# Weight preparation behind the experts: loads and ternary rounding in the experts' tail, transposes partly between the first scores

## The reference

```
x += tanh(g_xattn[0]) * L0_xattn(layernorm(x), ctx)   # small attention
x += tanh(g_ffn[0])   * L0_ffn(layernorm(x))          # 64 routed experts, top 4, and 2 shared ones
x += tanh(g_xattn[1]) * L1_xattn(layernorm(x), ctx, ctx)  # 32 query heads of 8, keys and values of ctx
x += tanh(g_ffn[1])   * L1_ffn(layernorm(x))          # rmsnorm, causal attention of 16 heads, gated MLP
x += tanh(g_xattn[2]) * L2_xattn(ctx, layernorm(x))
x += tanh(g_ffn[2])   * L2_ffn(layernorm(x))          # ternary weights
x += tanh(g_xattn[3]) * L3_xattn(layernorm(x), ctx, ctx)  # 16 heads, projection Wc
x += tanh(g_ffn[3])   * L3_ffn(layernorm(x))          # soft mixture of experts
```

## Time and profile before

| | us |
|---|---|
| median of 3 runs | 1261.07 (1260.91 to 1263.65) |
| profiled execution | 1259.72, of which the span 1257.9 |
| busy in the span | PE 1044.5, PEld 667.9, DVE 742.0, ACT 524.7, POOL 328.0 |
| stretch of the weight preparation and the start of attention A | about 403 to 454 |

### The profile page before, as it was taken

One profiled execution on the slowest core, in us unless ns is written; L12 is line 12 of the kernel. 1 busy time (PEld: TensorE's weight loads), 2 busy tenths in 40 slices (PEclk: granted clock), 3 DMA queues, 4 the chain that ended last, 5 costly groups with the idle time before them and its releaser, 6 DMA issues.

```text
span 1257.9 us, 18978 instructions
## 1 busy us (share of the span) xinstructions
PE 1044.5 (83%) x6622; PEld 667.9 (53%) x6625; DVE 742.0 (59%) x1684; ACT 524.7 (42%) x883; POOL 328.0 (26%) x626
## 2 busy tenths in 40 slices
PE   4369999999998688877988899991464878999997
PEld 2258888888887432333455435650322434566575
DVE  6875554444443577787565212479697674784743
ACT  1223233333333556565554430233473553544543
POOL 7023434343333456435343200001310300000000
PEclk9659999999999768999999899795686799999999
DMA  6101121111310400000000300002000000000000
GB/s 151 42 1 39 38 50 42 46 46 42 117 25 1 142 2 2 2 3 2 3 3 4 118 1 1 1 1 51 1 2 1 3 2 1 1 9 1 9 10 9
DMA packets 62444, 32.09 MB, mean 26 GB/s; under 512 B 47104, under 2 KB 61072, under 8 KB 62112
## 3 DMA queue, kind: packets, MB, share of 16 engines
q1 hardware_dynamic: 62368, 31.10, 9.3%
HBM read 29.64 MB, written 1.05 MB: 24 GB/s over the span
## 4 chain that ended last, share of the span: by engine, by line
PE 69%; DVE 21%; ACT 4%; issue 3%; POOL 1%; DMA 1%; SPq 0%; POOLq 0%; DVEq 0%; ACTq 0%; PEldq 0%
PE bank L762 16%; PE bank L778 8%; PE bank L874 4%; PE bank L1160 3%; DVE mx L2272 3%; PE bank L989 2%; PE bank L1341 2%; PE bank L957 2%; PE bank L1358 2%; PE bank L919 2%; PE bank L1343 2%; PE bank L1092 2%; PE bank L1140 2%; PE bank L1193 1%; DVE mxc L2272 1%
## 5 line engine op out<-in xcount | busy, mean ns | idle before, releaser
L2272 DVE TENSOR_REDUCE mx<-bank 128x2 f32<-128x512 f32 (+1 forms) x176 | 117.7, 689 | 71.0 <-PE bank L1092 35.1
L1708 ACT ACTIVATE prob<-bank 128x512 f32<-128x512 f32 x176 | 102.9, 597 | 89.3 <-PE bank L1140 62.1
L1520 ACT ACTIVATE hhi<-hh 128x512 fp32r<-128x512 f32 x72 | 45.5, 632 | 153.1 <-DVE hh L2108 140.4
L2104 DVE TENSOR_TENSOR hu<-bank,sg 128x512 f32<-128x512 f32 x64 | 44.3, 692 | 97.1 <-PE bank L762 97.1
L762 PE MATMUL bank<-xh,wh 128*128 128x512 f32 x288 | 91.6, 399 | 0.0
L762 PE MATMUL bank<-xh,wl 128*128 128x512 f32 x288 | 90.5, 395 | 0.0
L762 PE MATMUL bank<-xlo,wh 128*128 128x512 f32 x288 | 90.1, 394 | 0.0
L2096 DVE TENSOR_TENSOR hlo<-hh,hhi 128x512 fp32r<-128x512 f32 x72 | 57.2, 794 | 50.7 <-ACT hhi L1520 50.7
L2704 POOL TENSOR_TENSOR wl<-wraw,wh 128x512 fp32r<-128x512 f32 x72 | 80.6, 1119 | 13.0 <-POOL wh L2701 13.0
L1585 ACT ACTIVATE sg<-bank 128x512 f32<-128x512 f32 x72 | 43.1, 598 | 61.9 <-PE bank L762 61.9
L762 PEld LDWEIGHTS bank<-xh,wh 128*128 128x128 f32 x288 | 54.6, 190 | 13.3 <-issue 0.3
(11 more groups left out here) (456 smaller groups left out, 2275.0 us busy)
## 6 DMA issues: line engine op xcount, KB each, us to landing
wraw<-in_L_ffn_wg_dram SPq DMA_DIRECT2D x64, 64.0 KB, 2.3
wraw<-in_L_ffn_wu_dram SPq DMA_DIRECT2D x64, 64.0 KB, 2.4
wraw<-in_L_ffn_wd_dram SPq DMA_DIRECT2D x32, 128.0 KB, 2.4
l_raw<-in_L_ffn_w_dram SPq DMA_DIRECT2D x2, 1024.0 KB, 6.8
mun<-in_L_ffn_mu_dram SPq DMA_DIRECT2D x1, 2048.0 KB, 7.6
xs<-in_x_dram SPq DMA_DIRECT2D x1, 1024.0 KB, 5.5
w1s<-in_L_ffn_W_dram SPq DMA_DIRECT2D x2, 512.0 KB, 7.7
stage<-in_L_ffn_W_in_base_dram SPq DMA_DIRECT2D x1, 1024.0 KB, 7.8
```

What stands on the lines that cost most here:

```text
L1520: return act.activation(dst, src, ACT.Copy, scale=scale)
L1708: act.activation(t.prob[k][:, :], bank[3 + n % 2][:, :], ACT.Exp).then_inc(S("probs"), 1)
L2104: tt(hu[k % 2][:, :], bank[4 + (n + 1) % 4][:, :], sg[k % 2][:, :], ALU.mult).then_inc(once("up_used"), 1)
L2272: V.reduce_max(out_, bank[n % 3][:, :].rearrange("p (h t) -> p h t", h=heads), AX, negate=True)\
```

## The change

- The stage tiles get room of their own behind the experts' tiles (the memory of the first stage), and SP loads all of them as soon as the last shared expert's load is issued; one semaphore, `stage_loaded`, counts all eight.
- ACT's loop is one turn shorter, the eight units of the tail are written out behind it, and the two sums of magnitudes stand before units 0 and 1. PE's product with ones stands in unit 1. DVE's scale stands in unit 2 and its six rounding passes one each behind units 2 to 7. `tern` moves to the memory of `at_f`.
- POOL's clearing memsets and the parts of the first keys no longer wait for the last `down`.
- The transposes use banks 3 to 5 in turn. The first twelve groups stand before the attention. Four more (wupT) stand in a new slot -4, behind `xn` on ACT. The eight of wdT stand one behind each `by_query` of slot -2, the twelve ternary ones two behind each of the first six of slot -1, and the product for `wa` behind the seventh.
- `prepared` and the last copies are waited for by the first `by_key` instead of ahead of the attention; DVE copies `wa` at the end of slot -1, behind the maxima.

The diff, cut to what the above names (`...` where lines are left out):

```diff
-        top[0] = region
-        top[0] += DC * TOKENS * 4
+        top[0] = after_experts + 8192
         stage = [sb(f"stage{k}", [P, 2048]) for k in range(4)]
         wo = sb("wo", [P, DC, D])
-        after_prep = max(top[0], after_experts + 8192)
-        top[0] = region
-        tern = [sb(f"tern{k}", [P, 2048], BF16) for k in range(2)]
+        after_prep = top[0]
...
+        tern_at = top[0]
         at_f = sb("at_f", [P, B, NT, D])
+        top[0] = tern_at
+        tern = [sb(f"tern{k}", [P, 2048], BF16) for k in range(2)]
...
+        PREP_BANKS = (3, 4, 5)
+        PREP_AT = {"first": range(12), (-4, 0): range(12, 16)}
+        for n in range(8):
+            PREP_AT[-2, n] = range(16 + n, 17 + n)
+            PREP_AT[-1, n] = range(24 + 2 * n, 26 + 2 * n) if n < 6 else range(30 + n, 31 + n)
+        assert PREP_AT[-1, 6] == range(len(PREP + PREPB), len(PREP + PREPB) + 1)
+        del PREP_AT[-1, 7]
+        def prep_bank(g):
+            return PREP_BANKS[g % len(PREP_BANKS)]
...
-            sp.wait_ge(once("hidden_used"), 2 * PAIRS + 4)
-            sp.wait_ge(once("experts_out"), 2 * HALVES)
+            sp.wait_ge(once("batch_arrived"), 3)
...
-            stg = once("stage_rest_loaded")
...
                     up((u + 1) // 2, (u + 1) % 2, T * 8 + u + 1, T * SLOTN + (u + 1) // 2, shared=True)
+                if u == 1:
+                    pe.wait_ge(once("abs_sums"), 2)
+                    mm(bank[4][:, 0:2], ones[:, :], st[:, 0:2], start=True, stop=True).then_inc(once("abs_total"), 1)
                 down(u // 2, u % 2, T * 8 + u, T * SLOTN + u // 2, last_pair=u // 2 == SLOTN - 1)
...
-            pe.wait_ge(once("xs_updated"), 4)
-            pe.wait_ge(once("abs_sums"), 2)
-            mm(bank[4][:, 0:2], ones[:, :], st[:, 0:2], start=True, stop=True).then_inc(once("abs_total"), 1)
-            pe.wait_ge(once("stage_loaded"), 5 * 16)
-            for g, (srcs, dst) in enumerate(PREP + PREPB):
-                if g >= 4:
-                    pe.wait_ge(once("prep_done"), g - 3)
-                if g == FIRST_STAGES:
-                    pe.wait_ge(once("stage_rest_loaded"), 3 * 16)
+            pe.wait_ge(once("stage_loaded"), 8 * 16)
+            def prepare(g):
+                if g == 0:
+                    pe.wait_ge(once("xs_updated"), 4)
+                if g >= len(PREP_BANKS):
+                    pe.wait_ge(once("prep_done"), g + 1 - len(PREP_BANKS))
                 if g == len(PREP):
                     pe.wait_ge(once("ternary"), 2)
-                for j, src in enumerate(srcs):
+                if g == len(PREP + PREPB):
+                    for m in range(DC):
+                        for cc in range(DC):
+                            last = mm(bank[prep_bank(g)][:, m * R:(m + 1) * R], wo[:, cc, m * P:(m + 1) * P], am[:, cc, :],
+                                      start=cc == 0, stop=cc == DC - 1)
+                    last.then_inc(once("wa_made"), 1)
+                    return
+                for j, src in enumerate((PREP + PREPB)[g][0]):
                     if g < len(PREP):
-                        last = pe.transpose(bank[g % 4][:, j * P:(j + 1) * P], src, ident[:, :])
+                        last = pe.transpose(bank[prep_bank(g)][:, j * P:(j + 1) * P], src, ident[:, :])
                     else:
-                        last = pe.transpose(bankb[g % 4][:, j * P:(j + 1) * P], src, identb[:, :])
+                        last = pe.transpose(bankb[prep_bank(g)][:, j * P:(j + 1) * P], src, identb[:, :])
                 last.then_inc(once("prep_made"), 1)
-            g = len(PREP + PREPB)
-            pe.wait_ge(once("prep_done"), g - 3)
-            for m in range(DC):
-                for cc in range(DC):
-                    last = mm(bank[g % 4][:, m * R:(m + 1) * R], wo[:, cc, m * P:(m + 1) * P], am[:, cc, :],
-                              start=cc == 0, stop=cc == DC - 1)
-            last.then_inc(once("wa_made"), 1)
-            pe.wait_ge(once("prepared"), 1)
-            pe.wait_ge(once("prep_done"), len(PREP + PREPB))
+            for g in PREP_AT["first"]:
+                prepare(g)
...
+                    if stream == "A" and n == 0:
+                        pe.wait_ge(once("prepared"), 1)
+                        pe.wait_ge(once("prep_done"), len(PREP + PREPB))
...
-                for sl in range(-3, S_ + (1 if stream == "A" else 3)):
+                for sl in range(-4, S_ + (1 if stream == "A" else 3)):
...
+                        if stream == "A":
+                            for g in PREP_AT.get((sl, k), ()):
+                                prepare(g)
...
-            with act.Fori(0, PAIRS // SLOTN) as t:
+            with act.Fori(0, E // 2 // SLOTN) as t:
                 for k in range(2 * SLOTN):
                     gate(k, t * 8 + k)
+            for k in range(2 * SLOTN):
+                if k < 2:
+                    if k == 0:
+                        act.wait_ge(once("l2_loaded"), 2 * 16)
+                    act.activation(tern[k][:, :], l2_raw[k][:, :], ACT.Abs, accum_out=st[:, k:k + 1]).then_inc(once("abs_sums"), 1)
+                gate(k, E + k)
...
+            act.wait_ge(once("ternary"), 2)
+            def prepared(g):
+                srcs, dst = (PREP + PREPB)[g]
                 act.wait_ge(once("prep_made"), g + 1)
-                src = (bank if g < len(PREP) else bankb)[g % 4]
+                src = (bank if g < len(PREP) else bankb)[prep_bank(g)]
                 copy(dst, src[:, 0:len(srcs) * P], scale=0.25 if g < DC else 1.0).then_inc(once("prep_done"), 1)
+            for g in PREP_AT["first"]:
+                prepared(g)
...
                     for k in range(8):
+                        if stream == "A":
+                            for g in PREP_AT.get((sl, k), ()):
+                                if g < len(PREP + PREPB):
+                                    prepared(g)
...
-            act.wait_ge(once("prepared"), 1)
...
+                if k == 2:
+                    dve.wait_ge(once("abs_total"), 1)
+                    step(ts(wdq[:, :], bank[4][:, 0:2], 1.0 / (F1 * D), 1e-5, ALU.mult, ALU.max))
+                    step(V.reciprocal(st[:, 2:4], wdq[:, :]))
                 rest_of_hidden(k, u)
+                if k >= 2:
+                    w = l2_raw[(k - 2) // 3][:, :]
+                    if k in (2, 5):
+                        step(ts(w, w, st[:, 2 + k // 5:3 + k // 5], -1.0, ALU.mult, ALU.max))
+                    elif k in (3, 6):
+                        step(ts(w, w, 1.0, ROUND, ALU.min, ALU.add))
+                    else:
+                        ts(tern[(k - 2) // 3][:, :], w, ROUND, None, ALU.subtract).then_inc(once("ternary"), 1)
...
-            dve.wait_ge(once("abs_total"), 1)
-            step(ts(wdq[:, :], bank[4][:, 0:2], 1.0 / (F1 * D), 1e-5, ALU.mult, ALU.max))
-            step(V.reciprocal(st[:, 2:4], wdq[:, :]))
-            for k in range(2):
-                w = l2_raw[k][:, :]
-                step(ts(w, w, st[:, 2 + k:3 + k], -1.0, ALU.mult, ALU.max))
-                step(ts(w, w, 1.0, ROUND, ALU.min, ALU.add))
-                ts(tern[k][:, :], w, ROUND, None, ALU.subtract).then_inc(once("ternary"), 1)
+            dve.wait_ge(once("xs_updated"), 4)
             stats_of(step, 8 ** -0.5, range(2 * T0))
             dve.sem_inc(S("ln_x"), 1)
             step(V.tensor_copy(l2wj[:, 1:P], l2wj[:, 0:1].broadcast_to([CD, P - 1])))
-            dve.wait_ge(once("wa_made"), 1)
-            step(V.tensor_copy(wa[:, :, :], bank[len(PREP + PREPB) % 4][:, 0:DC * R].rearrange("p (m r) -> p m r", m=DC)))
-            dve.sem_inc(once("prepared"), 1)
-            dve.wait_ge(once("xs_updated"), 4)
...
+                        if (stream, sl, k) == ("A", -1, 7):
+                            dve.wait_ge(once("wa_made"), 1)
+                            step(V.tensor_copy(wa[:, :, :], bank[prep_bank(len(PREP + PREPB))][:, 0:DC * R].rearrange("p (m r) -> p m r", m=DC)))
+                            dve.sem_inc(once("prepared"), 1)
...
             end_loop(3, [n for n in STAGES[2] if n])
-            pool.wait_ge(once("hidden_used"), 2 * PAIRS + 4)
             step = Steps(pool, S("pool_step_b"))
```

9 lines of the change are left out of this document (1 added, 8 removed).

## The result

Over seven runs each, the changed kernel took 1252.75 us in the median (1242.13 to 1257.46) and the kernel before 1262.70 (1257.37 to 1264.85): a ratio of 0.9922, 95% interval 0.9892 to 0.9951. At 1261 us that is −9.8 us (−6.2 to −13.6), where −11.8 was forecast. A second set gave 0.9908 (0.9890 to 0.9926). It is faster, inside the range, and by the sign and about the size that the sum gave. But the sum came near the time partly by luck: one term was twice as large as forecast, and only a small part of that was made up by other terms.

A forecast was written before the change was run, and what follows sets the result against it. No single engine bounds the program; between experts and attention a relay runs steps serially that need not be. −16.4 + 5.6 − 1.0 = −11.8 us gives 1249.3 us; own range 1246.5 to 1252, 8-in-10 range 1244.5 to 1256.5.

The forecast's parts named there:

- Tail: Experts' last eight units: rounding passes fit into VectorE's idle time at 0; TensorE's small product with ones costs +0.4 us.
- xn: Normalising x ahead of the attention, behind statistics and twelve copies instead of all 36: from 435.61 to 419.2, −16.4 us.
- Groups 12 to 15 behind xn: wupT copies on ScalarE, 2.1 us, fit while GpSimd splits queries; xn to first scores stays 7.75 us.
- The filled stretch: First scores to first keys-by-queries product, with 21 groups added: 10.7 to 16.3 us, +5.6; bounds 11.9 and 19.2.
- The moved work: Transposes and product for wa added on TensorE between the first score tiles: 2.7 + 3.5 + 1.1, together 7.3 us.
- The part at the fast clock: Later part of the score tiles with added transposes: TensorE, busy without a pause, speeds up, 1.1 us less.
- half clock throughout: Rival, chance 0.14: score tiles with added transposes stay at 0.50, cost +8.5, nothing gained later; −7.9, 1253.2 us.
- What follows: Attention behind the first keys-by-queries product: TensorE may arrive warm, 2.2 us less; half taken, −1.0 us.
- Lockstep: Rival, chance 0.07: ScalarE's copies and three banks pace the score tiles with added transposes, +10 there; −6.4, 1254.7 us.
- The tail did not pay: Rival, chance 0.04, claimed the opposite: rounding passes overrun the experts' last units by 10.8 us, eating the gain; 1260.
- A colder attention: Rival, chance 0.06: clock rises fall otherwise and later attention groups run at 0.50; slower, 1262 to 1273 us.
- Fast clock throughout: Rival, chance 0.12: score tiles with added transposes cost +3 and the later 2.2 us come whole; −15.6, 1245.5 us.

The follow-up runs named there:

- x8: Changed kernel with the six rounding passes put back behind the updates of x, ahead of the statistics; 1261.12 us, 0.9988 of the kernel before.
- x5: The kernel before the change, run again without edit for a second profile; 1263.3 us.
- x6: Changed kernel plus 18 idle TensorE products in the pause between the twelve first groups and the first scores; 1247.41 us, 0.9883 of the kernel before.
- x3: Changed kernel with each transpose of the 20 groups in the two filled slots issued twice; 1249.08 us, 0.9895 of the kernel before.
- x2: Changed kernel with all 36 transposed groups and the product for wa ahead of xn again, rounding and loads still in the tail; 1254.3 us, 0.9934 of the kernel before.

## Why the prediction was right in size, and where it was wrong

**Tail, forecast +0.4 and the passes at no cost: right.** From the hlo that starts at 361.05 to the end of the update of x it took 51.07 us before and 51.43 in the changed kernel with the same start, +0.36; in x8, which has the tail without the passes, 51.29. So the passes cost 0.1 us and the rest of the change in the tail 0.2. The passes did meet GpSimd's memsets, and both engines paid at times. VectorE's rows, and then GpSimd's:

```profile
398.38 2.62 DVE L2153 TENSOR_SCALAR l_raw<-l_raw,st 128x2048 f32<-128x2048 f32 x1
401.04 0.69 DVE L2142 TENSOR_TENSOR hh<-bank,sg 128x512 f32<-128x512 f32 x1
402.49 0.69 DVE L2122 TENSOR_TENSOR hlo<-hh,hhi 128x512 fp32r<-128x512 f32 x1 [0.76 <-ACT hhi L1536]
403.10 1.67 DVE L2155 TENSOR_SCALAR l_raw<-l_raw 128x2048 f32<-128x2048 f32 x1
```

```profile
398.12 1.80 POOL L2751 MEMSET kstx<- 128x2048 bf16 x1
399.99 1.38 POOL L2753 MEMSET vstx<- 128x384 f32 x1
```

The longest pass took 2.62 us, and the same pass in x8, with no memset beside it, 1.28. It started in one memset and ended in the next; the small memset beside its end took 1.38 us, in the kernel before 0.42. hh followed without idle time, and the slack took what the pass was longer. By the Trainium skill, SBUF — State Buffer, section "Who interferes with whom", a VectorE tensor_scalar in a two-port mode and a GpSimd instruction block each other for a whole instruction. The trace agrees: the pass was 1.3 us longer, and GpSimd's small memset 1.0.

**xn, forecast −16.4: right, and a little better.** The forecast has the tail's +0.4 in it, so behind the update it is −16.8. Measured from 23.49 to 6.14 us behind the update it is −17.35 (−18.5 from the 24.65 of x5). The forecast had VectorE's and ScalarE's routes end nearly together, at 418.6 and 419.2; the copies came 0.8 us sooner than the statistics, so VectorE alone decided. That was the better of its bounds, which put xn 6.1 us behind the update.

**Groups 12 to 15 behind xn, forecast free: right.** 7.70 against 7.75 us to the first scores.

**The filled stretch, forecast +5.6 and at most +8.5: wrong, it was +11.8.** This is the step that failed, in three of its terms.

*The moved work.* The sum took 16/64 of 10.8 us for the fp32 transposes, 3.5 for the bf16 ones and 1.1 for wa, all from rows of a time when the granted clock was mostly 1.00, and laid them onto a stretch that the same rows show at 0.50. By the starts of its rows the changed kernel took 4.8 us for the 16 fp32 transposes there, 4.0 for the 32 bf16 ones and 1.8 for wa: 10.6 instead of 7.3.

*The work that was there.* The sum put it at TensorE's old busy time, 8.86. In the changed kernel it took 10.9: the scores of a tile take 0.51 to 0.54 us before the transposes behind them start. In the kernel before, at the same 0.50, three tiles that follow each other directly took 444.30 − 443.36 = 0.94 us, 0.31 each, and the later ones went at the pace of VectorE's maxima:

```profile
443.36 1.01 PE L1092 MATMUL bank<-kTx,qT 48*128 48x256 bf16 x6 [0.88 <-DVE kTx L2236]
444.30 1.04 PE L1022 MATMUL bank<-identb,qst 128*128 128x128 bf16 x8
445.27 3.79 PE L1092 MATMUL bank<-kTx,qT 48*128 48x256 bf16 x14
```

Why scores take longer between transposes is not shown.

*The part at the fast clock.* The 1.1 us taken off for it did not come.

With the wait for the copy of wa (0.94, forecast 1.2) the terms are 10.9 + 10.6 + 0.9 = 22.4 us. The case named for a low clock, "half clock throughout", used the same fast-clock prices in its upper bound of 19.2 us, so no case held the 22.5. Half clock was what happened in three profiles of three, and had been given a chance of 0.14.

**The clock in it: the reasoning for a rise was wrong.** TensorE was busy without a pause for 22 us and the clock stayed at 0.50. It had fallen at 423.7, in the second of two pauses of 1.75 and 1.35 us ahead of the turns of queries and keys. Filling the pauses kept it up (x6), more work behind them brought it up after 5.6 us (x3). Why 22 us of dense work did not bring it up is open. The Trainium skill, TensorE: Matmul & The Clock Gate, section "Part 4: PE-mode transpose", says that transposes do not engage the fast clock. The stretch agrees with it; 425 to 430 of the kernel before and x3, where only more transposes were added, speak against it. So the rule named the right danger here, but it does not hold for all transposes.

**The wait for wa: right.** 0.94 us ahead of the first keys-by-queries product.

**What follows, forecast −1.0: the sign is right, for another reason.** In the changed kernel the first prob products come 4.63 us behind the first keys-by-queries product, before 5.76, in every profile of each, at half clock in both. What went is a wait for GpSimd's parts of the next maxima. The kernel before has it behind the product (454.04):

```profile
455.84 0.20 POOL L2818 CAST mstr<-mx 128x16 bf16<-128x16 f32 x1 [2.74 <-DVE mx L2272]
457.00 0.39 PE L1103 MATMUL bank<-identb,mstr 128*24 128x128 bf16 x2 [1.03 <-POOLq L2822]
```

and the changed kernel (product at 450.74) does not:

```profile
450.59 0.20 POOL L2847 CAST mstr<-mx 128x16 bf16<-128x16 f32 x1 [7.95 <-DVE mx L2298]
452.57 0.39 PE L1113 MATMUL bank<-identb,mstr 128*24 128x128 bf16 x2
```

The product now stands behind the copy of wa, and so behind the last maximum; GpSimd's parts begin 0.15 us ahead of it instead of 1.80 behind it. The wait has in the main moved to the other side of the product, where it is the 0.94 us for wa. It has nothing to do with the filling: x2, with nothing in the stretch, has the same 4.63. From the first scores to the first prob products it is 16.4 us before, 27.1 in the changed kernel and 17.3 in x2.

So that piece is −1.1. Against the earlier trace rows, the products themselves were still slow once and then fast:

```profile
455.37 1.93 PE L1173 MATMUL bank<-prob,vstx 128*32 128x512 f32 x8
...
459.37 1.07 PE L1173 MATMUL bank<-prob,vstx 128*32 128x512 f32 x8
```

**The sum.** Tail +0.4, xn −17.35, stretch +11.8, the maxima's wait −1.1: −6.3 at the first prob products, by profiles with one start (−7.5 against x5, where xn stood later); −11.8 was forecast and −9.8 and −11.6 were timed. The stretch was 6.2 us dearer than forecast; xn made up 0.6 of that and what follows 0.1. The other 3.5 to 5 us that bring the timed difference near the forecast lie behind and are open, so that much of the agreement is luck. The three profiles of the changed kernel have 802.3 us behind the product in the mean and the two of before 804.1, but single ones scatter by 3 us. Whole profiled executions with the same start differ by 8.0 us (1259.72 to 1251.72, early) and 7.8 (1263.3 to 1255.5, the mean of two, late).

**Its own signs.** xn near 419 (420.6, and 418.6 with the early start) and the first scores near 427 (428.3, 426.3) came. The first keys-by-queries product near 443 (450.7, 448.8) and a granted clock above 0.5 in the stretch ahead of it did not.

**The rivals.** Lockstep is refuted by x6. The tail did not pay. A colder attention is not seen on balance. "Fast clock throughout", forecast at 1245.5, is what x6 made of the kernel with 18 idle products: 1247.41. Its +3 for the stretch was given without a sum; at 0.95 in the mean it was 14.93 − 10.69 = +4.2.
